# A two-layer graph network on one Trainium2 core: the load ring's 1 MB chunks moved as two transfers of 512 KB, each with its own semaphore

## The chip, the cores and the metric

The kernel runs on one core of a Trainium2 chip. The metric is the device time of one execution in microseconds (us); of several runs the median is given. Inside a core, TensorE (PE) multiplies, VectorE (DVE) and ScalarE (ACT) work on elements, GpSimd (POOL) and SyncE (SP) issue transfers here, and 16 DMA engines move data between HBM and the on-chip memory of 128 partitions.

## The reference

x is 8192 x 128, adj is a dense 8192 x 8192 matrix, all float32. Two residual graph layers are computed, and both need all of adj:

```python
# layer 0
adj_hat = adj + eye
d = 1.0 / sqrt(sum(adj_hat, axis=1))
h = relu((adj_hat * d[:, None] * d[None, :]) @ (x @ W0) + b)
x = layernorm(x + h)
# layer 1
s = x @ W1
o = relu(s + adj @ s + x @ Wself)
o = o - mean(o, axis=0)
o = o / sqrt(mean(sum(o * o, axis=1) + 1e-6))
out = layernorm(x + o)
```

Layer 0 needs the row sums of adj (for d) before it can scale the rows that it multiplies, and layer 1 needs layer 0's result.

## The kernel before

adj is cut into 8 x 8 blocks of 1024 x 1024, and each block into Q = 4 chunks of 1 MB: 128 partitions by 2048 floats, 8 KB per partition. A chunk has JB = 2 slices of 1024 columns (BLK). The host lays adj out twice, transposed within the blocks (`adjT`, for the products) and plain (`adjN`, for row sums), each chunk contiguous.

There are three kinds of chunks in one list, `chunks`, whose order every engine follows:

- "keep": a diagonal block's chunk, loaded into the tile `kept` (the memory of `o1`, so the profile calls it o). It is summed by column by VectorE (L680, L684) and later multiplied from there. It has its own semaphore per q.
- "sum": a chunk of `adjN` whose row sums are taken, by ScalarE (`sum_rows`, L497, in place with an accumulator, one instruction per slice) if `chunk.act`, else by VectorE (L670, one reduction of the whole chunk).
- "mul": a chunk of `adjT` that is multiplied. Float32 is split in two: for each slice ScalarE writes hi (L491), VectorE lo = raw - hi (L664), and TensorE runs hi and lo against the stationary halves rhi and rlo (L959, L961, L965: six matmuls of 128x512 for one layer, twelve for two), and in phase 1 four more per slice that sum columns (L941). rhi (L485) and rlo (L662) are made once per chunk. There are DEEP = 4 hi and lo tiles; ScalarE may write the hi of slice n when slice n - 4 is multiplied (semaphore slice_multiplied).

**Stages.** Stage 0 loads row block 0: 4 kept chunks and 28 sum chunks. Stage k (1 to 7) multiplies the kept chunks and column k - 1 for the rows from k on, each product chunk beside one sum chunk or kept chunk of row k, for as long as there are some, and ends with a tail of 8 product chunks (TAIL), in which the degrees of row block k are found (close_sums, L975; turn_degree, L985, which writes pA; first_product, L995). That is phase 1, up to about 780 us. Phase 2 runs blocks for both layers from one load, phase 3 (from about 1400 us) the rest of layer 1. Then the last normalisations follow.

**The ring.** Sum chunks, and product chunks that aren't kept, go through ring buffers of 1 MB: four of their own (raw0 to raw3) and, while nothing else needs that memory, s34 and s56 (in s1) and z23, z45, z67 (in zr); the profile calls these s and zr. Nine serve in stage 0 and the first stages, fewer later, four in phase 2, seven in phase 3. A planner gives each ring chunk the buffer that was freed first, `chunk.load` (how many loads that buffer has had) and `chunk.after`, the semaphore and count that say that the former chunk in the buffer is used up: ("split", n) when VectorE has made lo of n slices, ("act", n) or ("dve", n) when n sum chunks are done. SP (L419, L426) issues all adj transfers in the list's order, and waits for `after` before each. A consumer waits for `landed(chunk)`. All of SP's transfers go on DMA queue q1. GpSimd loads blocks of x transposed (512 KB, 4 KB per partition) into s1 once per stage, on queue q0.

Of the 532 adj transfers on q1, 32 are of kept chunks and 500 go through the ring.

Of the kernel before, what the change touches and what calls it, by code (L numbers as in the profile page):

```python
# [49 lines left out]
def graph_kernel(nc, x, xT, adjT, adjN, W0, b_rows, W1, Wself, out):  # L50
# [10 lines left out]
    BLK = 1024  # L61
    NB = N // BLK
    assert NB == 8
    Q = 4
    JB = 2
# [95 lines left out]
    for chunk in chunks:  # L161
        if chunk.kind == "mul":
            chunk.base = slices
            slices += JB
            chunk.stats = tuple(range(stats, stats + len(chunk.layers)))
            stats += len(chunk.layers)
            chunk.freed = ("split", slices)
            visits[chunk.visit].end = slices
        elif chunk.kind == "sum" and chunk.act:
            act_sums += 1  # L170
            chunk.freed = ("act", act_sums)
        elif chunk.kind == "sum":
            dve_sums += 1
            chunk.freed = ("dve", dve_sums)

# [6 lines left out]
    for chunk in chunks:  # L184
        if chunk.kind == "keep" or chunk.cached:
            continue
        phase = visits[chunk.visit].phase if chunk.kind == "mul" else 1
        if phase == 3 and not late:
            late = True
            free_buffers.extend((b, ("split", chunk.base)) for b in LATE)  # L190
        while phase < 3 and free_buffers[0][0] in BORROWED and (
                phase == 2 or chunk.stage > BORROWED[free_buffers[0][0]]):
            free_buffers.popleft()
        chunk.buf, chunk.after = free_buffers.popleft()
        loads[chunk.buf] += 1
        chunk.load = loads[chunk.buf]
        free_buffers.append((chunk.buf, chunk.freed))
        if phase == 1:
            phase1_last[chunk.buf] = chunk.freed
# [2 lines left out]
        for s in chunk.stats:  # L202
            stat_end[s] = chunk.base + JB
    kept_end = {(c.row, c.q): c.base + JB for c in chunks if c.cached}
    act_sums_of = [sum(1 for c in chunks if c.kind == "sum" and c.act and c.stage <= k) for k in range(NB)]


    free = {0: None, 1: None}
# [63 lines left out]
    with ctx:  # L272
# [58 lines left out]
        pD = pb("pD")  # L331
        sums = [pC, pD]

        loaded = {b: sem(f"loaded_{b}") for b in raw}
        kept_in = [sem(f"kept_in{q}") for q in range(Q)]
        consts_in = sem("consts_in")
        ident_zero = sem("ident_zero")
# [61 lines left out]
        def groups(ap):  # L399
            return ap.rearrange("p (g f) -> p g f", f=P)  # L400

        def landed(chunk):

            if chunk.kind == "keep" or chunk.cached:
                return kept_in[chunk.q], 16 * (chunk.row + 1)
            return loaded[chunk.buf], 16 * chunk.load

        def slice_of(chunk, j):
            if chunk.kind == "keep" or chunk.cached:
# [3 lines left out]
        @block.sync  # L413
        def _(sp):
            for chunk in chunks:
                if chunk.kind == "keep":
                    if chunk.row > 0:
                        sp.wait_ge(slice_split, kept_end[chunk.row - 1, chunk.q])
                    sp.dma_start(kept[:, chunk.q * TILE:(chunk.q + 1) * TILE],  # L419
                                 adjT[chunk.row, chunk.col, chunk.q]).then_inc(kept_in[chunk.q], 16)  # L420
                elif chunk.buf:
                    if chunk.after:
                        by, count = chunk.after
                        sp.wait_ge(raw_free[by], count)
                    src = adjN if chunk.kind == "sum" else adjT
                    sp.dma_start(raw[chunk.buf], src[chunk.row, chunk.col, chunk.q]).then_inc(loaded[chunk.buf], 16)  # L426

        @block.gpsimd
        def _(pool):
            pool.dma_start(w0[:, :], W0).then_inc(consts_in, 16)  # L430
            pool.dma_start(w1[:, :], W1).then_inc(consts_in, 16)
            pool.dma_start(t1[:, 0:P], Wself).then_inc(consts_in, 16)
            pool.dma_start(rows[:, :], b_rows).then_inc(consts_in, 16)
            pool.dma_start(xT_blk, xT[:, 0:BLK]).then_inc(xT_in, 16)
            pool.memset(ident[:, :], 0.0).then_inc(ident_zero, 1)
            pool.wait_ge(ident_zero, 1)
            pool.affine_select(out=ident[:, :], in_=ident[:, :], compare_op=ALU.not_equal, fill=1.0,
                               base=0, pattern=[[-1, P]], channel_multiplier=1).then_inc(ident_ready, 1)
            for k in range(1, NB):
                pool.wait_ge(y_done, k * H)  # L440
                pool.dma_start(xT_blk, xT[:, k * BLK:(k + 1) * BLK]).then_inc(xT_in, 16)
            pool.wait_ge(y_done, NB * H)
            pool.wait_ge(sums_closed, NB)
            for b in ("s34", "s56"):
                by, count = phase1_last[b]
                pool.wait_ge(raw_free[by], count)
            for k in FINAL_ROWS:
                pool.dma_start(groups(s1[:, k * BLK:(k + 1) * BLK]),
                               x[k * BLK:(k + 1) * BLK, :].rearrange("(g p) f -> p g f", p=P)).then_inc(x_in[k], 16)

            def store(k):
                pool.dma_start(out[k * BLK:(k + 1) * BLK, :].rearrange("(g p) f -> p g f", p=P),
                               groups(zr[:, k * BLK:(k + 1) * BLK])).then_inc(out_done, 16)

            def store_act(k):
                pool.wait_ge(act_normed, k + 1)
                store(k)

            def store_dve(i):
                pool.wait_ge(dve_normed, i + 1)  # L460
                store(i + NACT)

            for k in range(NACT - 1):
                store_act(k)
            for i in range(NB - NACT - 1):
                store_dve(i)
            store_act(NACT - 1)
            store_dve(NB - NACT - 1)
            pool.wait_ge(out_done, 16 * NB)

        @block.scalar
        def _(act):
            S = nc.scalar

            def split_hi(chunk):
                for l, s in zip(chunk.layers, chunk.stats):
                    src = (zr, s1)[l]
                    if l == L0:
                        act.wait_ge(z_ready, chunk.col + 1)
                    else:  # L480
                        act.wait_ge(s1_ready, ORDER[chunk.col] * H + chunk.q // 2 + 1)
                    if s >= DEEP:
                        act.wait_ge(slice_multiplied, stat_end[s - DEEP])
                    at = chunk.col * BLK + chunk.q * JB * P
                    S.activation(rhi[s % DEEP][:, :], src[:, at:at + JB * P], ACT.Copy)  # L485
                act.wait_ge(*landed(chunk))
                for j in range(JB):
                    n = chunk.base + j
                    if n >= DEEP:
                        act.wait_ge(slice_multiplied, n - DEEP + 1)  # L490
                    S.activation(hi[n % DEEP][:, :], slice_of(chunk, j), ACT.Copy).then_inc(hi_ready, 1)  # L491

            def sum_rows(chunk):
                act.wait_ge(*landed(chunk))
                for j in range(JB):
                    g = chunk.col * BG + chunk.q * JB + j
                    ins = S.activation(slice_of(chunk, j), slice_of(chunk, j), ACT.Copy,  # L497
                                       accum_out=rsum[chunk.row % 2][:, g:g + 1])
                ins.then_inc(act_summed, 1)

            def read_sums(k):
                act.wait_ge(sums_closed, k + 1)
# [132 lines left out]
        def _(dve):  # L635
# [29 lines left out]
                                 hi[n % DEEP][:, :].bitcast(f32)).then_inc(slice_split, 1)  # L665

            def sum_rows(chunk):
                dve.wait_ge(*landed(chunk))
                g = chunk.col * BG + chunk.q * JB
                V.tensor_reduce(rsum[chunk.row % 2][:, g:g + JB],  # L670
                                raw[chunk.buf].rearrange("p (g j) -> p g j", g=JB),
                                AX.X, ALU.add).then_inc(dve_summed, 1)

            def sum_kept(chunk):
                k, q = chunk.row, chunk.q
                dve.wait_ge(*landed(chunk))
                if q == 0:
                    if k > 0:
                        dve.wait_ge(sums_closed, k)
                    V.tensor_add(colsum, slice_of(chunk, 0), slice_of(chunk, 1)).then_inc(col_step, 1)  # L680
                    return
                for j in range(JB):
                    dve.wait_ge(col_step, k * (JB * Q - 1) + q * JB + j - 1)
                    V.tensor_add(colsum, colsum, slice_of(chunk, j)).then_inc(col_step, 1)  # L684
# [20 lines left out]
            def make_z(k):  # L705
# [2 lines left out]
                dk = d[:, k * BG:(k + 1) * BG]  # L708
                for b, rows in (("z23", (2, 3)), ("z45", (4, 5)), ("z67", (6, 7))):
                    if k in rows:  # L710
                        by, count = phase1_last[b]
                        dve.wait_ge(raw_free[by], count)
                step(V.reciprocal(dk, sq[:, :]))
                newton(step, dk, deg[:, :], nw[:, :])
# [386 lines left out]
```

## Time and profile before

| | us |
|---|---|
| median of 3 runs | 1932.26 |
| lowest, highest | 1929.6, 1933.44 |
| the profiled execution | 1931.12 |
| its span in the trace | 1929.3 |
| TensorE busy in it | 1742.8 (90%) |
| VectorE busy | 1522.3 (79%) |
| ScalarE busy | 1283.0 (66%) |
| adj moved on q1 | 557.88 MB in 76608 packets |

The profile is one execution on the core. Times in it are microseconds from the span's start. An engine's idle time is put down to the instruction or the landing that ended it ("<-"). The mean DMA rate is 297 GB/s, but it is spread unevenly: the page's 40 slices show 420 GB/s in most of the first eight and 131 to 200 in the middle. A timeline merges instructions that follow one another without idle time ("x2"). A packet is one piece of a transfer; a transfer over 128 partitions has 128 data packets and 16 that signal its end, one for each DMA engine, so 144.

### The profile page before, as it was taken

The numbers are of one execution on the slowest core, as the hardware profiler recorded it, in microseconds if no ns is written. First come the engines' busy times: TensorE is split into PE (matmuls) and PEld (weight loads), VectorE is DVE, ScalarE is ACT, GpSimd is POOL, SyncE is SP. The second block draws the span as 40 slices with busy tenths as digits, with TensorE's granted clock in tenths as the row PEclk, the third lists the DMA queues.
The fourth block names the chain that finished last, engine by engine and source line by source line (L and its number), as shares of the span: only waits on it lengthen the run. The fifth ranks groups of instructions, "written<-read, shape, count | busy, mean of one in ns | idle before, by whom it ended". The sixth has DMA issues, their size and how long they took to land.

```text
span 1929.3 us, 21167 instructions
## 1 busy us (share of the span) xinstructions
PE 1742.8 (90%) x7682; PEld 1411.9 (73%) x7682; DVE 1522.3 (79%) x2139; ACT 1283.0 (66%) x1885; POOL 21.5 (1%) x34
## 2 busy tenths in 40 slices
PE   1089999999999999888999999999989999999983
PEld 0068778878787877766778788788868778888872
DVE  4488688697878789975777575575589999999986
ACT  3577787677866656644554554454468888888875
POOL 0000000000000000100000000000000000000001
PEclk7589999999999999998999999999999999999995
DMA  9999999989899577743444545545579999999953
GB/s 399 421 422 421 421 370 421 401 358 389 335 373 370 198 293 320 258 175 131 173 160 168 197 159 193 194 173 189 190 292 395 354 369 381 375 376 391 375 193 87
DMA packets 80296, 572.07 MB, mean 297 GB/s; under 512 B 8960, under 2 KB 8960, under 8 KB 12096
## 3 DMA queue, kind: packets, MB, share of 16 engines
q1 hardware_dynamic: 76608, 557.88, 73.2%
q0 software_dynamic: 3584, 12.85, 2.1%
q8 instruction: 60, 0.98, 0.2%
q14 instruction: 44, 0.36, 0.0%
HBM read 566.49 MB, written 4.19 MB: 296 GB/s over the span
## 4 chain that ended last, share of the span: by engine, by line
PE 72%; DVE 15%; DMA 6%; ACT 4%; issue 2%; SPq 0%; POOL 0%; ACTq 0%
PE acc L959 20%; PE acc L961 20%; PE acc L965 20%; DVE lo L664 8%; PE pC L941 4%; DMA s<-in_adjN 4%; PE pD L941 4%; ACT hi L491 1%; DVE rlo L662 1%; DMA raw<-in_adjT 1%; DMA zr<-in_adjN 1%; DVE s L670 1%; DVE s L684 1%; PE pC L1021 1%; PE pD L1022 1%
## 5 line engine op out<-in xcount | busy, mean ns | idle before, releaser
L959 PE MATMUL acc<-hi,rhi 128*128 128x512 f32 x2048 | 823.6, 402 | 61.9 <-DVE lo L664 42.5
L961 PE MATMUL acc<-lo,rhi 128*128 128x512 f32 x2048 | 804.4, 393 | 0.0
L491 ACT ACTIVATE hi<-raw 128x1024 fp32r<-128x1024 f32 x530 | 547.3, 1055 | 143.8 <-PE pD L941 79.9
L965 PE MATMUL acc<-hi,rlo 128*128 128x512 f32 x2048 | 636.5, 392 | 0.0
L664 DVE TENSOR_TENSOR lo<-raw,hi 128x1024 fp32r<-128x1024 f32 x530 | 625.3, 1218 | 12.0 <-ACT hi L491 12.0
L959 PEld LDWEIGHTS acc<-hi,rhi 128*128 128x128 f32 x2048 | 388.2, 190 | 171.0 <-DVE lo L664 68.0
L961 PEld LDWEIGHTS acc<-lo,rhi 128*128 128x128 f32 x2048 | 388.3, 190 | 82.9 <-issue 5.0
L965 PEld LDWEIGHTS acc<-hi,rlo 128*128 128x128 f32 x2048 | 387.7, 189 | 83.0
L662 DVE TENSOR_TENSOR rlo<-zr,rhi 128x256 fp32r<-128x256 f32 x256 | 107.9, 422 | 264.5 <-ACT hi L491 264.0
L485 ACT ACTIVATE rhi<-zr 128x256 fp32r<-128x256 f32 x256 | 104.3, 407 | 197.2 <-PE acc L965 196.4
L491 ACT ACTIVATE hi<-zr 128x1024 fp32r<-128x1024 f32 x184 | 193.8, 1060 | 43.4 <-PE pD L941 22.4
L664 DVE TENSOR_TENSOR lo<-zr,hi 128x1024 fp32r<-128x1024 f32 x184 | 216.7, 1217 | 2.1 <-ACT hi L491 2.1
L662 DVE TENSOR_TENSOR rlo<-s,rhi 128x256 fp32r<-128x256 f32 x256 | 107.3, 419 | 6.4 <-ACT hi L491 4.7
L485 ACT ACTIVATE rhi<-s 128x256 fp32r<-128x256 f32 x256 | 102.7, 401 | 2.8 <-PE acc L965 2.8
L497 ACT ACTIVATE raw<-raw 128x1024 f32<-128x1024 f32 x70 | 73.0, 1045 | 30.9 <-DMA raw<-in_adjN 30.9
L491 ACT ACTIVATE hi<-s 128x1024 fp32r<-128x1024 f32 x62 | 65.3, 1059 | 38.1 <-PE pD L941 36.6
L941 PE MATMUL pC<-hi,pick 128*128 128x512 f32 x224 | 88.6, 395 | 0.0
L941 PE MATMUL pD<-hi,pick 128*128 128x512 f32 x224 | 88.2, 394 | 0.0
L941 PE MATMUL pC<-lo,pick 128*128 128x512 f32 x224 | 88.0, 393 | 0.0
L941 PE MATMUL pD<-lo,pick 128*128 128x512 f32 x224 | 87.9, 392 | 0.0
L664 DVE TENSOR_TENSOR lo<-s,hi 128x1024 fp32r<-128x1024 f32 x62 | 73.8, 1218 | 6.8 <-ACT hi L491 6.8
L491 ACT ACTIVATE hi<-o 128x1024 fp32r<-128x1024 f32 x64 | 66.2, 1053 | 16.6 <-PE pD L941 12.6
(136 smaller groups left out, 1096.4 us busy)
## 6 DMA issues: line engine op xcount, KB each, us to landing
raw<-in_adjT SPq DMA_DIRECT2D x265, 1024.0 KB, 5.0
zr<-in_adjT SPq DMA_DIRECT2D x92, 1024.0 KB, 6.0
raw<-in_adjN SPq DMA_DIRECT2D x53, 1024.0 KB, 16.4
o<-in_adjT SPq DMA_DIRECT2D x32, 1024.0 KB, 11.0
s<-in_adjT SPq DMA_DIRECT2D x31, 1024.0 KB, 12.6
zr<-in_adjN SPq DMA_DIRECT2D x30, 1024.0 KB, 19.3
s<-in_adjN SPq DMA_DIRECT2D x29, 1024.0 KB, 18.5
s<-in_xT POOLq DMA_DIRECT2D x8, 512.0 KB, 7.7
```

The lines of the kernel that those rows point to most:

```text
L485: S.activation(rhi[s % DEEP][:, :], src[:, at:at + JB * P], ACT.Copy)
L491: S.activation(hi[n % DEEP][:, :], slice_of(chunk, j), ACT.Copy).then_inc(hi_ready, 1)
L497: ins = S.activation(slice_of(chunk, j), slice_of(chunk, j), ACT.Copy, accum_out=rsum[chunk.row % 2][:, g:g + 1])
L662: V.tensor_sub(rlo[s % DEEP][:, :], (zr, s1)[l][:, at:at + JB * P], rhi[s % DEEP][:, :].bitcast(f32))
L664: V.tensor_sub(lo[n % DEEP][:, :], slice_of(chunk, j), hi[n % DEEP][:, :].bitcast(f32)).then_inc(slice_split, 1)
L670: V.tensor_reduce(rsum[chunk.row % 2][:, g:g + JB], raw[chunk.buf].rearrange("p (g j) -> p g j", g=JB), AX.X, ALU.add).then_inc(dve_summed, 1)
L684: V.tensor_add(colsum, colsum, slice_of(chunk, j)).then_inc(col_step, 1)
L941: last = T.matmul(sums[h][:, :], to, mov[n % DEEP][:, h * HALF:(h + 1) * HALF], start=False, stop=False, skip_group_check=True)
L959: T.matmul(banks[h][:, :], a, hi[n % DEEP][:, part], start=(opens and j == 0), stop=False, skip_group_check=True)
L961: T.matmul(banks[h][:, :], a, lo[n % DEEP][:, part], start=False, stop=False, skip_group_check=True)
L965: last = T.matmul(banks[h][:, :], b, hi[n % DEEP][:, part], start=False, stop=end, skip_group_check=True)
L1021: T.matmul(pC[:, j * P:j * P + P], t2[:, j * P:j * P + P], w1[:, :], start=True, stop=True)
```

## The change

Each ring chunk is now moved by two transfers of 128x1024 floats, 512 KB, 4 KB per partition, one for each slice. Each half of each buffer has a semaphore of its own (`loaded[buf, j]`). `chunk.after` and `chunk.freed` become one entry per slice: SP waits for the slice that stood in that half before it issues the half. For product chunks the first half is freed when VectorE has made lo of its first slice. ScalarE's sums signal after each slice, so counts of act_summed double. VectorE's reduction still takes the whole chunk: it waits for both halves, and frees both at its end. ScalarE waits for a half in front of each slice, where it waited once per chunk. Kept chunks, their semaphores, and the order of `chunks` are as before.

```diff
-            chunk.freed = ("split", slices)
+            chunk.freed = tuple(("split", chunk.base + j + 1) for j in range(JB))
...
-            act_sums += 1
-            chunk.freed = ("act", act_sums)
+            act_sums += JB
+            chunk.freed = tuple(("act", act_sums - JB + j + 1) for j in range(JB))
...
-            chunk.freed = ("dve", dve_sums)
+            chunk.freed = (("dve", dve_sums),) * JB
...
-        loaded = {b: sem(f"loaded_{b}") for b in raw}
+        loaded = {(b, j): sem(f"loaded_{b}_{j}") for b in raw for j in range(JB)}
...
-                    if chunk.after:
-                        by, count = chunk.after
-                        sp.wait_ge(raw_free[by], count)
                     src = adjN if chunk.kind == "sum" else adjT
-                    sp.dma_start(raw[chunk.buf], src[chunk.row, chunk.col, chunk.q]).then_inc(loaded[chunk.buf], 16)
+                    for j in range(JB):
+                        if chunk.after:
+                            by, count = chunk.after[j]
+                            sp.wait_ge(raw_free[by], count)
+                        part = slice(j * BLK, (j + 1) * BLK)
+                        sp.dma_start(raw[chunk.buf][:, part],
+                                     src[chunk.row, chunk.col, chunk.q][:, part]).then_inc(loaded[chunk.buf, j], 16)
...
-                act.wait_ge(*landed(chunk))
                 for j in range(JB):
+                    act.wait_ge(*landed(chunk, j))
                     n = chunk.base + j
...
             def sum_rows(chunk):
-                act.wait_ge(*landed(chunk))
                 for j in range(JB):
+                    act.wait_ge(*landed(chunk, j))
...
-                ins.then_inc(act_summed, 1)
+                    ins.then_inc(act_summed, 1)
...
             def sum_rows(chunk):
-                dve.wait_ge(*landed(chunk))
+                for j in range(JB):
+                    dve.wait_ge(*landed(chunk, j))
```

SP's queue in stage 1, where products (in_adjT) and sums (in_adjN) alternate; s1 and zr are the borrowed buffers. Before:

```order
L426 DMA raw0<-in_adjT 128x2048 [waits slice_split]
L426 DMA raw1<-in_adjN 128x2048 [waits slice_split]
L426 DMA raw2<-in_adjT 128x2048 [waits slice_split]
L426 DMA raw3<-in_adjN 128x2048 [waits slice_split]
L426 DMA s1<-in_adjT 128x2048 [waits act_summed]
```

and in the changed kernel:

```order
L428 DMA raw0<-in_adjT 128x1024 [waits slice_split] x2
L428 DMA raw1<-in_adjN 128x1024 [waits slice_split] x2
L428 DMA raw2<-in_adjT 128x1024 [waits slice_split] x2
L428 DMA raw3<-in_adjN 128x1024 [waits slice_split] x2
L428 DMA s1<-in_adjT 128x1024 [waits act_summed] x2
```

The order is the same; each row has become two transfers of half the width, each behind a wait of its own.

ScalarE in stage 1, a product chunk, a sum chunk and the next product chunk. Before:

```order
L485 ACTIVATE rhi0<-zr 128x256 [waits slice_multiplied,z_ready]
L491 ACTIVATE hi0<-raw0 128x1024 [waits slice_multiplied,loaded_raw0]
L491 ACTIVATE hi1<-raw0 128x1024 [waits slice_multiplied]
L497 ACTIVATE raw1,s1<-raw1 128x1024 [waits loaded_raw1]
L497 ACTIVATE raw1,s1<-raw1 128x1024
L485 ACTIVATE rhi1<-zr 128x256 [waits slice_multiplied,z_ready]
L491 ACTIVATE hi2<-raw2 128x1024 [waits slice_multiplied,loaded_raw2]
```

and in the changed kernel:

```order
L488 ACTIVATE rhi0<-zr 128x256 [waits slice_multiplied,z_ready]
L494 ACTIVATE hi0<-raw0 128x1024 [waits slice_multiplied,loaded_raw0_0]
L494 ACTIVATE hi1<-raw0 128x1024 [waits slice_multiplied,loaded_raw0_1]
L500 ACTIVATE raw1,s1<-raw1 128x1024 [waits loaded_raw1_0]
L500 ACTIVATE raw1,s1<-raw1 128x1024 [waits loaded_raw1_1]
L488 ACTIVATE rhi1<-zr 128x256 [waits slice_multiplied,z_ready]
L494 ACTIVATE hi2<-raw2 128x1024 [waits slice_multiplied,loaded_raw2_0]
```

No instruction moves; each second slice has a wait on its own half.

## Rows read from the trace of the kernel before

**Rows 1.** Busy time by stretch; the columns are in the first line.

```profile
core 0: us, PE busy (x) PEld busy (x) DVE busy (x) ACT busy (x) POOL busy (x), PEclk, DMA share, GB/s
...
144.70:193.00 48.30, 48.17 (x211) 39.10 (x210) 38.94 (x41) 37.22 (x56) 0.00 (x0) 1.00 1.01 420
...
241.00:289.00 48.00, 44.36 (x192) 35.56 (x191) 40.87 (x48) 38.85 (x60) 0.53 (x1) 1.00 0.90 369
...
1000.00:1350.00 350.00, 345.59 (x1560) 283.72 (x1559) 222.22 (x381) 175.33 (x289) 0.00 (x0) 1.00 0.49 180
...
1400.00:1830.00 430.00, 417.37 (x1818) 338.92 (x1817) 421.64 (x520) 369.87 (x475) 0.00 (x0) 0.99 0.94 367
```

**Rows 2.** ScalarE in order of time: start, us, what, idle before and its end.

```profile
169.57 2.01 ACT L491 ACTIVATE hi<-raw 128x1024 fp32r<-128x1024 f32 x2 [2.65 <-DMA raw<-in_adjT]
...
209.31 2.01 ACT L491 ACTIVATE hi<-raw 128x1024 fp32r<-128x1024 f32 x2 [2.66 <-DMA raw<-in_adjT]
...
211.80 2.01 ACT L491 ACTIVATE hi<-raw 128x1024 fp32r<-128x1024 f32 x2 [0.17 <-DMA raw<-in_adjT]
```

**Rows 3.** The chain that ended last, 190 to 211 us: start, us, what.

```profile
190.46 18.83 DMA raw<-in_adjT
209.31 1.07 ACT hi L491
210.41 0.42 DVE rlo L662
210.83 1.15 DVE lo L664
```

**Rows 4.** DMA queues, 94 to 102, then 50 to 100 us: packets, MB, share.

```profile
q1 hardware_dynamic: 391, 2.83, 85.1%
q0 software_dynamic: 144, 0.52, 16.4%
...
q1 hardware_dynamic: 2815, 20.55, 98.8%
q0 software_dynamic: 144, 0.52, 2.6%
```

**Rows 5.** DMA queue and issues of kept chunks, 0 to 209.3 us.

```profile
q1 hardware_dynamic: 11760, 85.71, 98.7%
...
o<-in_adjT SPq DMA_DIRECT2D x8, 1024.0 KB, 14.9
```

**Rows 6.** Lone transfers: 645 to 665, 718 to 730, 260 to 268 us.

```profile
q1 hardware_dynamic: 432, 3.15, 42.9%
...
q0 software_dynamic: 144, 0.52, 14.7%
...
s<-in_adjT SPq DMA_DIRECT2D x1, 1024.0 KB, 4.8
```

**Rows 7.** SP's issues in order of time: start, us, what, count.

```profile
6.09 7.01 SPq L426 DMA_DIRECT2D zr<-in_adjN  x3
...
203.19 0.33 SPq L426 DMA_DIRECT2D s<-in_adjN  x1
```

**Rows 8.** The DMA queue from 268 to 336.5 us, and ScalarE at its end.

```profile
q1 hardware_dynamic: 3853, 28.16, 99.4%
...
336.46 1.06 ACT L491 ACTIVATE hi<-raw 128x1024 fp32r<-128x1024 f32 x1 [1.50 <-DMA raw<-in_adjT]
```

**Rows 9.** The DMA queue, 1500 to 1800 us, and TensorE at 1600 us.

```profile
q1 hardware_dynamic: 15286, 111.34, 94.9%
...
1599.87 0.39 PE L959 MATMUL acc<-hi,rhi 128*128 128x512 f32 x1
...
1601.23 0.39 PE L959 MATMUL acc<-hi,rhi 128*128 128x512 f32 x1
```

**Rows 10.** Who waited for whom, 640 to 780 us: total, times, longest.

```profile
ACT hi L491 <- DMA raw<-in_adjT: 7.3, 4, 2.4
...
PE acc L959 <- DVE lo L664: 1.2, 4, 0.5
```

More of the change, by code:

```diff
@@ L189, in graph_kernel @@
             late = True
-            free_buffers.extend((b, ("split", chunk.base)) for b in LATE)
+            free_buffers.extend((b, (("split", chunk.base),) * JB) for b in LATE)
         while phase < 3 and free_buffers[0][0] in BORROWED and (
@@ L204, in graph_kernel @@
     kept_end = {(c.row, c.q): c.base + JB for c in chunks if c.cached}
-    act_sums_of = [sum(1 for c in chunks if c.kind == "sum" and c.act and c.stage <= k) for k in range(NB)]
+    act_sums_of = [sum(JB for c in chunks if c.kind == "sum" and c.act and c.stage <= k) for k in range(NB)]
     free = {0: None, 1: None}
@@ L400, in groups, with landed @@
             return ap.rearrange("p (g f) -> p g f", f=P)
-        def landed(chunk):
+        def landed(chunk, j):
             if chunk.kind == "keep" or chunk.cached:
                 return kept_in[chunk.q], 16 * (chunk.row + 1)
-            return loaded[chunk.buf], 16 * chunk.load
+            return loaded[chunk.buf, j], 16 * chunk.load
         def slice_of(chunk, j):
@@ L444, in _ @@
             for b in ("s34", "s56"):
-                by, count = phase1_last[b]
+                by, count = phase1_last[b][-1]
                 pool.wait_ge(raw_free[by], count)
@@ L675, in sum_kept @@
                 k, q = chunk.row, chunk.q
-                dve.wait_ge(*landed(chunk))
+                dve.wait_ge(*landed(chunk, 0))
                 if q == 0:
@@ L710, in make_z @@
                     if k in rows:
-                        by, count = phase1_last[b]
+                        by, count = phase1_last[b][-1]
                         dve.wait_ge(raw_free[by], count)
```

## The prediction

> **What bounds the kernel now.** I read the table by stretches first [rows 1]. From 145 to 193 us, as in every stretch up to 241 us, the DMA engines are full: a share of 1.01 at 420 GB/s, which is 1.0486 MB every 2.49 us. From 241 to 289 us the share is 0.90 [rows 1], and from there on the DMA engines are full only for a while in each stage. From 1000 to 1350 us the DMA share is 0.49 and TensorE is busy for 345.59 of 350 us; from 1400 to 1830 us TensorE (417 of 430 us) and VectorE (422) are full, and DMA has 0.94 [rows 1].
>
> A full DMA does not yet mean that the end waits for it, so I read next what ScalarE, the first consumer of most chunks, waits for. From 150 to 209 us it stands at a product chunk once in 19.9 us for 2.65 us, and it is always the landing that ends the wait [rows 2]; 169.57 to 209.31 us is 39.74 us for 16 chunks, 2.48 us each, the pace of the DMA. The chain of waits agrees: a landing issued at 190.46 us is followed by hi, rlo and lo of that slice, and so by TensorE [rows 3]. The wait at 211.80 us is 0.17 us [rows 2] and is the last one of stage 1. So the time up to 209.3 us is the DMA's, and later TensorE's and VectorE's chains carry it. What the change does to the time is read from these first 209 us.
>
> **The price of a smaller transfer.** Every ring transfer had 8 KB per partition; now two have 4 KB each, in 128 pieces plus 16 completions each (144 packets in both cases). The kernel already has transfers of exactly the new shape: x^T, 512 KB in rows of 4 KB, which lands among ring transfers. From 94 to 102 us, q0's 144 packets took 16.4% of 16 x 8 us, 20.99 engine-us; over 16 engines 1.312 us, 2.624 us for a pair. q1's 391 packets took 85.1%, 108.9 engine-us, so 144 of them took 2.507 us per engine [rows 4]. The difference is +0.117 us per chunk. From 50 to 100 us the same working gives 2.60 against 2.527 us, +0.073 us, and the rounding of the 2.6% makes that +0.02 to +0.125 [rows 4]. I take +0.09 us per chunk, between the two, and keep 0.02 and 0.125 as ends. Below nothing the price can't be, since the same bytes go in more packets. The far end is a lone transfer: from 718 to 730 us q0's 144 packets took 14.7% of 192 us, 3.53 us for a pair, where three lone 8 KB transfers took 2.86 us each [rows 6]; a lone transfer's first pieces take long, and that goes away in a stream, as 2.86 against 2.507 shows, so I give this end no weight in the sum.
>
> The Trainium skill (DMA: Bandwidth & Descriptors, section "Why small descriptors are slow") has about 3 cycles of overhead per packet, at the 850 MHz that the page states. Eight more data packets per engine would then be 28 ns per chunk by this estimate, near the lower end of the rows, and the delay below would be 2.1 us instead of 6.7.
>
> **How many chunks pay.** By 209.3 us q1 had moved 85.71 MB, 81.7 transfers of 1.0486 MB, and 8 of them are kept chunks, which are not split [rows 5]: 73.7 ring chunks. 73.7 x 0.09 = 6.6 us later landing of the chunk on which TensorE hangs at 209.3 us.
>
> **What half a chunk earlier gives back.** The chunk's first half now lands one half, 2.58/2 = 1.29 us, ahead of its second. ScalarE makes hi of the first slice at once, and TensorE at 212 us hangs on just that slice [rows 3]. The second slice is in time: it comes 1.29 us behind, while the first takes TensorE 2.3 us (ten matmuls at about 0.23 us, by the pace of [rows 9]). So 1.3 us comes back, once, since the waits before it are one and the same bound. Net: 6.6 - 1.3 = +5.3 us.
>
> **Buffers freed by the slice** (SP waits for half a buffer). As long as the DMA queue never runs empty, an earlier issue lands nothing earlier: 0 until 209 us. Behind that, what SP waits for is a slot, and consumers wait for landings almost nowhere, so it is 0 there too; it is what could cover part of the next point.
>
> **The second full stretch.** From 268 to 336.5 us the DMA is at 99.4% again and moved 28.16 MB, 26.9 chunks, 4 of them kept [rows 8]. At 336.46 us ScalarE waits 1.50 us for a landing [rows 8]. 22.9 x 0.09 = 2.1 us later, less 1.3 us for the half: 0.8 us more wait. TensorE doesn't see it: ScalarE may start hi when the slice four back is multiplied, which leaves three slices of 2.3 us, 6.9 us, for a chain of hi, rlo and lo of 1.07 + 0.42 + 1.15 us [rows 3]; that is a cover of 4.2 us, of which 1.50 is used. 0 us.
>
> **The last phase.** TensorE's slices start 1.36 us apart (1599.87 and 1601.23 us), 2.72 us per chunk [rows 9]; the DMA would need 2.58. From 1500 to 1800 us it moved 111.34 MB [rows 9], 106 chunks in 300 us, one in 2.83 us on the mean. The cover is 0.14 us per chunk within a run of slices, which the chunks in store bridge, and 0.25 us on the mean, gone only at a price of 0.34 us. 0 us.
>
> **Issues and waits.** SP issues 500 transfers more. An issue takes 0.33 us in the steady part [rows 7], two in 2.58 us. The eleventh to thirteenth of the first issues take 7.01 us together without a wait on a semaphore [rows 7]: SP is held when some ten transfers are outstanding. Twice the transfers for the same bytes reach that at half the bytes, about 5 MB, which is still 13 us of work for the DMA; what is held behind it on SP (kept chunks too) could not land earlier anyway. 0 us. ScalarE gets one wait more per chunk, on a landing that in TensorE's part is long past: its two hi of a chunk already have a passed wait between them, and none of their starts pays for it. The sums of ScalarE signal per slice instead of per chunk, as hi does already. VectorE's sums wait for both halves, and free nothing earlier. 0 us for each.
>
> **Sum.** The profiled execution took 1931.12 us (span 1929.3); +5.3 gives 1936.4. It lies 1.1 us under the median of 1932.26, so the forecast on the median is 1937.6 us, +0.27%.
>
> **Rivals.**
> A, not slower: the price of a packet in a full stream is at the low end, 0.02 to 0.065 us per chunk. 1.5 to 4.8 us less 1.3: +0.2 to +3.5, 1932.5 to 1935.8 us, 1934 in the middle. For it: the rounding of the 2.6% row [rows 4]. Against it: the narrower window, 0.117. It decides at (3.9 + 1.3)/73.7 = 0.07 us.
> B, faster: the low price, and the half landing pays where the ring is short. From 640 to 780 us ScalarE waits for landings four times, 7.3 us in all [rows 10]; if each were on the path, 4 x 1.3 = 5.2 us come back, 1927 to 1931 us. Against it: TensorE waits for VectorE's lo there for 1.2 us in all [rows 10], so little can be had.
> C, slower by more: the full stretches of stages 2 to 4 start with less data in store, and each adds its own 2.1 us: +2 to +6 on top, 1940 to 1944 us. It decides when the cover of 2.7 us at 336 us is gone. Against it: stage 2's extra wait is worked out at 0.8 us.
> D: the price is over 0.34 us and the last phase runs at the DMA's pace; at 0.45 the first 209 us cost 73.7 x 0.45 - 1.3 = 32 us, and the 164 chunks of the last phase 0.11 each, 18 more: about 1982 us. Against it: both windows of [rows 4].
> E: what a transfer costs beyond its bytes is not hidden. A lone 1 MB lands 4.8 us after its issue [rows 6] and takes 2.49 in the stream; if each of the 74 added transfers cost the 2.3 us between them, 170 us: 2100 us. The Trainium skill (DMA: Bandwidth & Descriptors, "Rules for kernel authors") says the like: at least 1 MiB per DMA for full bandwidth. Against it: nine transfers are outstanding in the stretch that matters, and the 512 KB transfers in [rows 4] show no such gap.
>
> **How the numbers follow.** Forecast 0.55, A 0.25, C 0.11, B 0.05, D 0.03, E 0.01. The range takes in A and the forecast's upper end (0.125 x 73.7 - 1.3 = +7.9, 1940.2) and C: 1932 to 1944 us. A measurement of this kernel tells about 0.2%, 3.9 us, from no change. Above 1936.1 us lie C, D, E and most of the forecast (0.50): 0.65. Within are A and the rest: 0.30. Faster 0.05.
>
> **What would show it.** In the changed kernel's profile: 421 GB/s of the first 240 us down to about 406; the landing that frees TensorE at the end of stage 1 at 214 to 216 us instead of 209.3; the step to pA (the degree turned) of stage 1 some 5 us later, and the same 5 us at each later stage, neither growing nor shrinking; issues of SP of 1.3 us each in the first 200 us. A bandwidth that stays at 421 GB/s would make me wrong towards A; a shift that grows from stage to stage, towards C; waits of ScalarE for landings behind 1400 us, towards D.

## The result, and the profile after

| | before | changed |
|---|---|---|
| median, us (8 runs each) | 1931.74 | 1936.61 |
| lowest to highest | 1929.6 to 1937.13 | 1935.84 to 1938.64 |
| span of the profiled execution | 1929.3 | 1934.9 |

The ratio is 1.0024, with a 95% interval of 1.0013 to 1.0035: 4.9 us slower, where +5.3 was forecast. The profiled spans differ by 5.6 us.

The same stretches of the changed kernel, with the columns of [rows 1]:

```profile
144.70:193.00 48.30, 46.69 (x196) 35.94 (x196) 36.94 (x41) 35.85 (x53) 0.00 (x0) 1.00 1.03 409
...
241.00:289.00 48.00, 44.29 (x201) 35.82 (x200) 39.87 (x48) 40.87 (x65) 0.53 (x1) 1.00 0.94 372
...
1000.00:1350.00 350.00, 345.59 (x1562) 283.68 (x1561) 222.55 (x382) 177.11 (x293) 0.00 (x0) 1.00 0.55 180
...
1400.00:1830.00 430.00, 415.95 (x1817) 337.70 (x1816) 419.35 (x517) 366.91 (x473) 0.00 (x0) 1.00 0.97 364
```

Up to 241 us the DMA engines are as full as before, with a share of 1.03, but move 409 GB/s instead of 420. TensorE is busy 46.69 of the 48.3 us from 144.7 us on, where it was 48.17 [rows 1]. In the last phase the DMA share rises from 0.94 to 0.97 at nearly the same rate; TensorE's busy time in that window differs by 1.4 us, with all its work shifted by some 5 us.

ScalarE in stage 1 of the changed kernel, answering to [rows 2] (start, us, what, idle before and what ended it):

```profile
173.43 1.06 ACT L494 ACTIVATE hi<-raw 128x1024 fp32r<-128x1024 f32 x1 [2.48 <-DMA raw<-in_adjT]
...
214.37 1.06 ACT L494 ACTIVATE hi<-raw 128x1024 fp32r<-128x1024 f32 x1 [2.47 <-DMA raw<-in_adjT]
215.65 1.06 ACT L494 ACTIVATE hi<-raw 128x1024 fp32r<-128x1024 f32 x1 [0.22 <-DMA raw<-in_adjT]
...
218.19 1.06 ACT L494 ACTIVATE hi<-raw 128x1024 fp32r<-128x1024 f32 x1 [0.19 <-DMA raw<-in_adjT]
```

and the chain that ended last there (start, us, what), answering to [rows 3]:

```profile
198.37 15.97 DMA raw<-in_adjT
...
214.37 1.07 ACT hi L494
...
215.46 0.43 DVE rlo L665
215.89 1.15 DVE lo L667
```

The landing that frees TensorE at the end of stage 1 has moved from 209.31 to 214.37 us, +5.06. The second half is waited for at 215.65 us, 1.28 us behind the first. The chain behind the first half is the one of [rows 3], with the same durations.

How the 5 us go on is read from the step that writes pA (the degree turned) near the end of a stage. Stages 1, 2, 3 and 7, before, in order of time (start, us, what):

```profile
227.79 1.84 PE L985 MATMUL pA<-ident,t 128*128 128x1 f32 x16
...
358.21 1.84 PE L985 MATMUL pA<-ident,t 128*128 128x1 f32 x16
...
470.33 1.84 PE L985 MATMUL pA<-ident,t 128*128 128x1 f32 x16
...
774.77 1.84 PE L985 MATMUL pA<-ident,t 128*128 128x1 f32 x16
```

and in the changed kernel:

```profile
232.84 1.84 PE L989 MATMUL pA<-ident,t 128*128 128x1 f32 x16
...
363.33 1.84 PE L989 MATMUL pA<-ident,t 128*128 128x1 f32 x16
...
477.09 1.84 PE L989 MATMUL pA<-ident,t 128*128 128x1 f32 x16
...
781.75 1.84 PE L989 MATMUL pA<-ident,t 128*128 128x1 f32 x16
```

The shifts are 5.05, 5.12, 6.76 and 6.98 us; at the end of the span it is 5.6. So nearly all is there by the end of stage 1. The 1.6 us that come in stage 3 and go again behind 780 us are of the clock; they have a part of their own below.

The price of the pieces: queue q1 and the 512 KB transfer on q0 from 94 to 102 us, then q1 in the full stretch from 20 to 95 us, changed, and last the same stretch before (packets, MB, share):

```profile
q1 hardware_dynamic: 756, 2.74, 85.7%
q0 software_dynamic: 144, 0.52, 16.6%
...
q1 hardware_dynamic: 8430, 30.72, 102.6%
...
q1 hardware_dynamic: 4343, 31.65, 101.4%
```

A transfer of 144 packets on q1 takes 0.857 x 128 / 756 x 144 / 16 = 1.306 us per engine, 2.61 us for a pair; the estimate from x^T's rows had been 2.60 to 2.62 [rows 4]. But the bytes came down by less than the packets' times: 30.72 against 31.65 MB in 75 us is a chunk in 2.56 instead of 2.485 us, +0.075 us, while the sum of packet times over the engines rose from 101.4% to 102.6% of the stretch. A sum over 100% means that packets of one engine overlap, and the shorter ones overlap a little more.

SP's issues in stage 0 of the changed kernel (start, us, what, count):

```profile
24.09 10.20 SPq L428 DMA_DIRECT2D raw<-in_adjN  x8
...
46.82 10.20 SPq L428 DMA_DIRECT2D raw<-in_adjN  x8
```

Eight issues take 10.20 us, 1.28 each, one landing: SP is held at its queue, as [rows 7] had shown for the first issues. The landings come in an unbroken stream all the same.

### The profile page after: what moved, and what is told of

Read it like the earlier page. It is cut to its first block, busy times and chain, and to the rows that moved or that the text cites. A ratio compares the mean times of both kernels' runs of the same rounds, so it can differ in the third digit from the quotient of the medians.

```text
span 1934.9 us, 22120 instructions
## 1 busy us (share of the span) xinstructions
PE 1739.9 (90%) x7682; PEld 1406.6 (73%) x7682; DVE 1523.0 (79%) x2139; ACT 1285.8 (66%) x1885; POOL 21.5 (1%) x34
## 4 chain that ended last, share of the span: by engine, by line
PE 68%; DVE 18%; DMA 8%; ACT 3%; issue 2%; SPq 1%; POOL 0%; ACTq 0%; DVEq 0%
PE acc L963 19%; PE acc L969 19%; PE acc L965 19%; DVE lo L667 9%; PE pC L945 4%; PE pD L945 4%; DMA raw<-in_adjT 3%; DMA raw<-in_adjN 3%; DVE rlo L665 1%; DVE s L688 1%; ACT hi L494 1%; DMA s<-in_adjN 1%; DMA zr<-in_adjN 1%; DVE s L674 1%; DVE ux L731 1%
## 5 line engine op out<-in xcount | busy, mean ns | idle before, releaser
L494 ACT ACTIVATE hi<-o 128x1024 fp32r<-128x1024 f32 x64 | 66.1, 1053 | 16.7 <-PE pD L945 12.6
## 6 DMA issues: line engine op xcount, KB each, us to landing
raw<-in_adjN SPq DMA_DIRECT2D x106, 512.0 KB, 15.2
zr<-in_adjN SPq DMA_DIRECT2D x60, 512.0 KB, 15.2
s<-in_adjN SPq DMA_DIRECT2D x58, 512.0 KB, 15.2
```

## Experiments

Two theories stood against each other. **P**: pieces of 4 KB land more slowly than pieces of 8 KB, the DMA's stream up to 215 us carries that to the end, and the half that is used early gives about a microsecond back. **N**: the number of transfers, with their end signals, issues and waits, is the price. Beside them, **L**: part of the price is paid in later stages. All ratios are against the kernel before, run on the same chip beside it; its medians there were 1932.5 us (runs 1 to 3), 1930.8 us (runs 4 and 8) and 1930.1 us (the rest). Beside the times stand places in one trace of each run. How far such a place scatters by itself can be read from runs 5 and 6, which repeat the first two stages of the changed kernel and of the kernel before: pA of stage 1 differs by 0.27 and 0.16 us from theirs.

**1. The change's transfers, consumed in whole chunks.** ScalarE waits for both halves, and both are freed at the chunk's end:

```diff
-            chunk.freed = tuple(("split", chunk.base + j + 1) for j in range(JB))
+            chunk.freed = (("split", slices),) * JB
...
                 for j in range(JB):
                     act.wait_ge(*landed(chunk, j))
+                for j in range(JB):
                     n = chunk.base + j
```

> The changed kernel's transfers (two of 512 KB for a ring chunk), but consumed as before: ScalarE waits for both halves before its first slice, and both halves are freed together at the chunk's end. Theory P (smaller pieces land more slowly, and half a chunk's earlier start gives 1.28 us back): nothing of the delay is given back, so +6.3 us on the kernel before, about 1938, with TensorE's gating hi of stage 1 at 215.6 us instead of 214.4. Rival G (slice-wise waits and frees are worth nothing, the +5 is all the transfers' price): same as the changed kernel, 1936.6. Rival W (the extra waits and signals cost the time, not the transfers): near the kernel before, under 1934.

Measured: 1.0022 (1.0014 to 1.0031), 1937.1 us. Its chain at the end of stage 1 (start, us, what):

```profile
197.94 15.93 DMA raw<-in_adjT
213.86 1.35 issue
215.22 1.07 ACT hi L495
...
216.31 0.43 DVE rlo L667
216.74 1.15 DVE lo L669
```

The first half has landed at 213.86 us, and hi starts 1.35 us later, at 215.22 us, when the second half is there. TensorE's slice follows at 217.93 us, against 217.08 in the changed kernel and 212.02 before [rows 3]. So the transfers alone cost 5.9 us at this place, and using the half early gave 0.85 us back. Run 5, whose first two stages are the changed kernel's, gives a second reading of that:

```profile
214.08 1.06 ACT L508 ACTIVATE hi<-raw 128x1024 fp32r<-128x1024 f32 x1 [2.47 <-DMA raw<-in_adjT]
215.36 1.06 ACT L508 ACTIVATE hi<-raw 128x1024 fp32r<-128x1024 f32 x1 [0.22 <-DMA raw<-in_adjT]
...
216.79 0.50 PE L977 MATMUL acc<-hi,rhi 128*128 128x512 f32 x1 [0.16 <-DVE lo L681]
```

Its TensorE starts this slice at 216.79 us, 1.14 us before run 1. So the half is worth 0.85 to 1.14 us, more than the scatter. The time is 4.2 us over the kernel before (2.7 to 6.0), less than the 6.3 expected; it can't tell 1.0022 from the change's 1.0024, so rival G falls by the traces alone. Rival W, under 1934 us, falls here by the time, and again in run 2, which has neither the waits nor the signals.

**2. One transfer of 1 MB per chunk, but in pieces of 4 KB.** The host lays adj out slice by slice, and the transfer picks both slices:

```diff
-                    sp.dma_start(raw[chunk.buf], src[chunk.row, chunk.col, chunk.q]).then_inc(loaded[chunk.buf], 16)
+                    sp.dma_start(raw[chunk.buf].rearrange("p (j c) -> p j c", j=JB),
+                                 src[chunk.row, chunk.col, chunk.q].rearrange("j p c -> p j c")).then_inc(loaded[chunk.buf], 16)
```

> The kernel before with one transfer of 1 MB and one wait per ring chunk, but with adj laid out in HBM slice by slice, so that each piece is 4 KB as in the change (kept chunks as before). Theory P: the size of the pieces is the price: full stretches at about 410 GB/s instead of 421, 73.7 chunks at +0.07 us, nothing given back: +5 to +6 us, 1937 to 1938. Rival N (the number of transfers, their end signals and SP's held issues are the price): 421 GB/s as before and +0, 1931.7.

Measured: 1.0022 (1.0013 to 1.0031), 1937.1 us. Its queue q1 from 20 to 95 us, and two landings that ScalarE waits for, sixteen chunks apart:

```profile
q1 hardware_dynamic: 7963, 30.71, 102.6%
...
173.94 2.01 ACT L492 ACTIVATE hi<-raw 128x1024 fp32r<-128x1024 f32 x2 [2.81 <-DMA raw<-in_adjT]
...
214.86 2.01 ACT L492 ACTIVATE hi<-raw 128x1024 fp32r<-128x1024 f32 x2 [2.82 <-DMA raw<-in_adjT]
```

30.71 MB in 75 us, as in the changed kernel, with half as many transfers and end signals (7963 packets instead of 8430). 40.92 us for 16 chunks is 2.558 us each, where [rows 2] give 39.74 us, 2.484 each: +0.074 us. The landing that gates TensorE is at 214.86 us, 5.55 us late; 73.7 chunks x 0.074 is 5.45. So the price comes without a second transfer: P stands, N falls. With two transfers the chunk is there at 215.22 (run 1), 215.36 (run 5) and 215.65 us (the changed kernel), 0.36 to 0.8 us later than here, although q1 has moved 83.33 to 83.39 MB by 209.3 us in all four. Up to 0.3 us of that is scatter. Whether the rest is a small price of the second transfer, no run with pieces of 4 KB settles; run 4, with pieces of 8 KB, has none. This trace also has the shift without the clock's part: its pA comes 5.53, 5.53, 5.49 and 5.49 us late in stages 1, 2, 3 and 7.

**3. Two transfers with pieces of 8 KB, lower and upper 64 partitions.**

```diff
-                    sp.dma_start(raw[chunk.buf], src[chunk.row, chunk.col, chunk.q]).then_inc(loaded[chunk.buf], 16)
+                    for j in range(JB):
+                        part = slice(j * (P // JB), (j + 1) * (P // JB))
+                        sp.dma_start(raw[chunk.buf][part, :],
+                                     src[chunk.row, chunk.col, chunk.q][part, :]).then_inc(loaded[chunk.buf, j], 16)
```

> The kernel before with each ring chunk in two transfers of 64 partitions, pieces of 8 KB as before, both waited for before the chunk is used, freed as a whole. Theory P: only the second set of 16 end signals is added; 420 to 421 GB/s in the full stretches, within 1 us of the kernel before. Rival N (the number of transfers): +5 to +6 us, about 410 GB/s.

Measured: six runs from 2444 to 2555 us, median 2487.5; the ratio of the three shortest is 1.275 (1.269 to 1.281), and the profiled one took 2542.8 us. Neither theory had that. From 20 to 95 us:

```profile
DMA packets 2529, 16.62 MB, mean 222 GB/s; under 512 B 501, under 2 KB 501, under 8 KB 501
...
q1 hardware_dynamic: 2529, 16.62, 101.7%
```

222 GB/s, with the engines as full as ever: 1.017 x 1200 us over 2028 pieces (2529 packets less 501 end signals) is 0.60 us a piece of 8 KB. The Trainium skill (SBUF — State Buffer, section "Door 1: The DMA port swizzle") says that the rate of a transfer depends on how many of the 16 ways into the memory its partitions reach, and by its table the lower 64 reach eight, with about 218 GB/s as their limit; the trace agrees within 2%, with 222. This run can't judge N; run 4 answers both questions.

**4. The same with even and odd partitions.**

```diff
-                        part = slice(j * (P // JB), (j + 1) * (P // JB))
+                        part = slice(j, P, JB)
```

> As the run with two transfers of 64 partitions each, but one takes the even and the other the odd partitions, instead of the lower and the upper half; pieces of 8 KB, both waited for. It answers what that run could not, whether a second transfer costs anything by itself. Theory U (there the pieces took twice as long because a transfer to one half of the partitions reaches half of the ways into the memory): here a piece takes 314 ns again, 420 GB/s, and the time is within 1.5 us of the kernel before (1930 to 1933). Rival M (two transfers of 64 partitions are slow as such, by how they are dealt to the 16 engines): about 2490 again. If the pieces are fine and it still comes out 5 us slower, the number of transfers has a price of its own.

Measured: 1.0001 (0.9991 to 1.0011), 1930.6 us. From 20 to 95 us:

```profile
DMA packets 4819, 31.62 MB, mean 422 GB/s; under 512 B 960, under 2 KB 960, under 8 KB 960
...
q1 hardware_dynamic: 4817, 31.60, 101.3%
```

422 GB/s, 0.315 us a piece of 8 KB (1215.6 us over 3857 pieces), with 960 end signals in place of 480. So two transfers of the same bytes cost nothing if their pieces stay at 8 KB, which speaks against N a second time, and rival M falls: what was wrong with the halves by partition was which partitions they were, not that there were two. By the table of the Trainium skill (SBUF — State Buffer, section "Door 1: The DMA port swizzle") each of these transfers reaches all sixteen ways. The rows read from HBM change together with the partitions, and no run parts the two.

**5. The change in stages 0 and 1 alone; 6. from stage 2 on alone.** A flag `chunk.cut` (its negation in run 6) chooses per chunk between the two halves and one whole transfer that is waited for and freed as before:

```diff
+        chunk.cut = chunk.kind != "mul" and chunk.stage <= 1 or chunk.kind == "mul" and 0 < chunk.stage <= 1
...
+                    if not chunk.cut:
+                        if chunk.after:
+                            by, count = chunk.after[-1]
+                            sp.wait_ge(raw_free[by], count)
+                        sp.dma_start(raw[chunk.buf],
+                                     src[chunk.row, chunk.col, chunk.q]).then_inc(loaded[chunk.buf, 0], 16)
+                        continue
```

> The change for the ring chunks of stages 0 and 1 alone; from stage 2 on, ring chunks move as one transfer of 1 MB, waited for and freed whole. Theory P: the whole price lies in the first 215 us: +5 us, 1936.6, with every later stage shifted by the same 5. Rival L (part of the price lies in the later full stretches of stages 2 to 4 or in the last phase): +2 to +4.

> The change for the ring chunks from stage 2 on alone. Theory P: no difference from the kernel before, within 1 us (1931 to 1932.5), since no landing gates TensorE behind 215 us: the waits of ScalarE that are left (2.5 us at 343 us in the changed kernel) are covered. Rival L: +1 to +3 us.

Measured: early alone 1.0029 (1.0017 to 1.0040), 1936.3 us; late alone 1.0004 (0.9995 to 1.0013), 1932.0 us. In the trace of the first the writes of pA are at 232.57, 363.05 and 476.80 us, +4.8, +4.8 and +6.5; the second has 227.95, 360.05, 472.29, that is +0.2, +1.8 and +2.0. Of the +6.5, and of the +1.8 and +2.0, 1.6 us are again the clock's (below). Run 6 has them in stage 2, where its granted clock is 0.94 and that of the kernel before 1.00 (columns of [rows 1]):

```profile
265.00:292.00 27.00, 25.22 (x102) 20.23 (x103) 23.33 (x24) 19.76 (x30) 0.00 (x0) 0.94 0.88 341
```

80 chunks are cut in run 5 and the other 420 in run 6. The pieces of the 420 cost the DMA engines time too, from 1000 to 1350 us 55.6% of it, where it was 48.8%, for the same 62.9 MB; no landing of theirs carries it to the end. So L falls by the traces: of the 2.2 us at pA of stage 7, 0.6 are left without the clock's part. The time alone would not exclude 1 to 2 us of it: run 6's interval reaches from -1.0 to +2.5 us.

**7. Four transfers of 256 KB per chunk**, pieces of 2 KB, two transfers to a half's semaphore:

```diff
+                        for h in range(H):
+                            part = slice(j * BLK + h * HALF, j * BLK + (h + 1) * HALF)
+                            sp.dma_start(raw[chunk.buf][:, part],
+                                         src[chunk.row, chunk.col, chunk.q][:, part]).then_inc(loaded[chunk.buf, j], 16)
```

> The change carried on: four transfers of 256 KB per ring chunk, 2 KB per partition, one semaphore per half. Theory P with a fixed price per piece: from 8 to 16 pieces per engine and chunk cost 0.075 us, so 32 pieces cost 0.22 in all: 74 x 0.22 = 16.5 us, less 1.3: +15 us, 1947, with 395 to 398 GB/s in the full stretches; the last phase needs 2.83 us per chunk and gets 2.71, so nothing is added there. Rival S (SP's issues, 0.33 us each and held when about ten transfers are outstanding, become the limit): over +25 us, and gaps in the full stretches. Rival H (the price is one of the second transfer, not of the pieces): +5 to +8.

Measured: 1.0097 (1.0083 to 1.0111), 1949.8 us: 18.7 us slower, where 15 were expected. q1 from 20 to 95 us, and a piece of the chain in stage 2:

```profile
q1 hardware_dynamic: 15907, 28.98, 105.3%
...
350.00 9.85 DMA raw<-in_adjT
359.87 1.07 ACT hi L495
```

28.98 MB in 75 us is 386 GB/s, 2.71 us a chunk: +0.23 us over the kernel before, as expected from a fixed price per piece (0.075 for 8 pieces more per engine and chunk, 0.225 for 24). The 395 to 398 GB/s of the expectation don't follow from its own price, which gives 388. Rivals S and H fall, the time lying between them and the stretch having no gap. pA is written at 244.50 us in stage 1, 16.7 us late; expected was 15.2. What had been left out is the second line of the chain: in stage 2 a landing gates TensorE again, at 359.87 us. That is rival C of the prediction, at three times the change's price. At 378.34 us stage 2 is 20.1 us late, 1.6 of the 3.4 between them being the clock's (below).

**8. Quarters in stages 0 and 1 alone.** The edit of 7 under the flag of 5.

> Four transfers of 256 KB per ring chunk in stages 0 and 1 alone, whole chunks from stage 2 on. With quarters everywhere the degree turned was 16.7 us late at the end of stage 1 and 20.1 at the end of stage 2. Theory C2 (the second full stretch came to gate TensorE there, by its own price of 0.2 us per chunk): the 3.4 us between the two are gone, except where a stretch at half clock falls in between (1.5 us); stage 1 at 244.5 us, stage 2 at 374.9 to 376.5, in all 1946.5. Rival (the loss behind stage 1 is of the clock or of the shifted meeting of the engines alone): stage 2 at 378 again, 1949.5.

Measured: 1.0099 (1.0084 to 1.0114), 1949.9 us; that total, 3.4 us over the expected one, can't be told from that of run 7. In the trace pA is written at 243.96 us in stage 1 and at 376.00 in stage 2, as expected, and no landing is waited for in between. Stage 2 takes 132.04 us here and 133.84 with quarters throughout, both with one stretch at half clock in them: the gating landing of stage 2 costs 1.8 us. The spans, 1947.2 against 1948.8 us, say the same; the timed runs are too few to.

**9. Only six chunks in halves**, the last two product chunks before the column sums close in stages 1 to 3 (the flag of 5 with another condition).

> The kernel before, with the change for six chunks alone: the last two product chunks before the column sums close in stages 1, 2 and 3, among them the one whose landing gates TensorE at 209.3 us. Theory P: the gating slice starts 1.24 us earlier and almost nothing is paid: -1.2 us, 1930.5. That is less than a measurement of the time can tell; the trace shows it: the hi at 209.31 us at 208.1, and the degree turned (writing pA) at 226.7 instead of 227.95. Rival G (the half is worth nothing): both as before.

Measured: 1.0003 (0.9994 to 1.0012). hi of the gating chunk and TensorE's first matmul on it (start, us, what):

```profile
208.29 1.06 ACT L508 ACTIVATE hi<-raw 128x1024 fp32r<-128x1024 f32 x1 [1.64 <-DMA raw<-in_adjT]
...
211.84 0.50 PE L977 MATMUL acc<-hi,rhi 128*128 128x512 f32 x1
```

hi starts 1.0 us earlier than at 209.31 [rows 2], but TensorE only 0.2 us earlier than at 212.02: pA is written at 227.60 instead of 227.79 us. TensorE was still at the slices before. Before this landing it had waited only for the 0.2 us between their end at 211.8 and 212.02, since its pace of 4.6 us for a product chunk is close to the DMA's 4.97 us for a product and a sum chunk. The expected 1.2 us were wrong; a lone half is worth what TensorE waits at that landing, not what the half lands ahead. With 0.16 us of scatter in pA, the 0.2 us gained can't be told from rival G.

No version beats the kernel before.

## Why the prediction was right, point by point

**What bounds the first 209 us.** Right: a slower stream came out as a later end, by 5.05 us at pA of stage 1, and the change in stages 0 and 1 alone makes the whole loss (run 5).

**The price of a piece.** The packets' own times were right (2.61 us a pair, 2.60 to 2.62 forecast), the price was a bit too high: 0.09 forecast, 0.070 by the rates of 409.5 and 421 GB/s, 0.074 by the landings of run 2. The step that was off is the division by 16 engines as if packets stood in line: they overlap, by 1.4% before and 2.6% after. The 3 cycles per packet of the Trainium skill (DMA: Bandwidth & Descriptors, section "Why small descriptors are slow"), 28 ns per chunk by the estimate in the prediction, would have given 0.8 us in all; 70 to 75 ns were measured, so here the measurement decides against it.

**The chunks that pay.** 73.7 fits: times 0.074 it is 5.45 us, and run 2 has 5.55, run 1 5.91 at the same place. Forecast were 6.6.

**What the half gives back.** Forecast 1.3 us, measured 0.85 (run 1 against the change) to 1.14 (run 1 against run 5). The first half does land 1.28 us ahead of the second. But the second half of the changed kernel lands at 215.65 us, that of run 5 at 215.36 and that of run 1 at 215.22, with the same 83.33 MB moved by 209.3 us in each. So the stream isn't slower: the 0.4 us are mostly the scatter of single landings, 0.29 us between the first two, which share this part of the program. Run 9 corrects the reason that the prediction gave, that TensorE hangs on the one slice at 212 us: it had waited 0.2 us for it, and the last halves alone gave no more. That the gain comes about because all product chunks are early, so that TensorE has no backlog of its own, fits runs 1 and 9 but wasn't tried by itself.

The forecast's +5.3 against 5.05 there is closer than its terms. Against run 1 the price is 0.7 us too high (6.6 for 5.91) and the half 0.45 too high (1.3 for 0.85), and the two errors partly cancel; that much of the closeness is luck. The median came out 1.0 us under the 1937.6 forecast, half of it because the kernel before has a median of 1931.74 over eight runs, where the forecast started from 1932.26.

**The second full stretch.** The wait was to grow from 1.50 us by 0.8; it is 2.46 us:

```profile
342.99 1.06 ACT L494 ACTIVATE hi<-raw 128x1024 fp32r<-128x1024 f32 x1 [2.46 <-DMA raw<-in_adjT]
```

and stage 2's shift is 5.12 us against stage 1's 5.05, so it stayed covered. Run 7 shows the cover's end: at a price of 0.23 us per chunk it is gone, and costs 1.8 us. By the prediction's own terms, 2.7 us of cover plus the 1.3 of the half over 22.9 chunks, it is gone at 0.17 us.

**The last phase.** ScalarE waits for no landing from 780 to 1830 us, as before. q1 moved 111.58 MB from 1500 to 1800 us against 111.34 [rows 9]:

```profile
q1 hardware_dynamic: 30647, 111.58, 98.7%
```

Its share rose from 94.9% to 98.7%, and no landing was waited for. With quarters (run 7) it is 103.8% there, and ScalarE waits for a landing twice from 780 to 1830 us, 2.8 us in all.

**Issues and waits.** The held issues were seen as foretold and cost nothing; run 4 has the issues doubled at no loss.

**Rivals.** A needed a price under 0.07 us, which it nearly has. The time says slower (4.9 us, interval 2.5 to 6.8), but the interval reaches into A's +0.2 to +3.5; what excludes A is the 5.05 us in the trace. B to E didn't come. One sign that the prediction named was misleading: "a shift that grows from stage to stage" was to point to C, and the shift did grow, by 1.6 us in stage 3, for another reason.

## What the runs showed that was not expected

**TensorE's clock adds or takes 1.6 us by stage.** From 401 to 411 us of the changed kernel, just behind the short stalls in which each stage begins, the granted clock is 0.83 on the mean; then 1.00. Busy times by stretch, with the columns of [rows 1]:

```profile
401.00:411.00 10.00, 8.22 (x30) 6.29 (x29) 9.70 (x12) 8.52 (x14) 0.00 (x0) 0.83 0.60 209
411.00:417.00 6.00, 6.00 (x28) 4.99 (x27) 3.00 (x4) 5.23 (x8) 0.00 (x0) 1.00 1.03 429
```

and the matmuls in it, four in order of time:

```profile
407.17 0.63 PE L945 MATMUL pC<-hi,pick 128*128 128x512 f32 x1
407.59 0.63 PE L945 MATMUL pC<-lo,pick 128*128 128x512 f32 x1
...
410.47 0.39 PE L945 MATMUL pC<-hi,pick 128*128 128x512 f32 x1
410.69 0.39 PE L945 MATMUL pC<-lo,pick 128*128 128x512 f32 x1
```

Two successive starts are 0.42 us apart at 407 us (the level of 1.2 GHz) and 0.22 to 0.23 us at 410 us (2.4 GHz). The kernel before has no such stretch there, but has one behind 836 us, where the changed kernel has none. Before, then changed:

```profile
836.00:846.00 10.00, 7.37 (x30) 5.49 (x28) 5.79 (x8) 5.70 (x10) 0.00 (x0) 0.88 0.55 210
```

```profile
843.00:852.00 9.00, 5.79 (x28) 4.26 (x26) 6.39 (x9) 5.97 (x10) 0.00 (x0) 1.00 0.68 237
```

TensorE is 5.18 us behind the kernel before at 405.08 us, ahead of the slow matmuls, and 6.75 us behind at 411.37. That is why the shift goes from 5.12 to 6.76 us in stage 3, and from 6.98 us at 805 us to 5.40 at 846 (the two additions into t, at 805.32 and 845.88 us before, 812.30 and 851.28 changed). Runs 6 to 9 have a clock under 1 between 269 and 290 us instead, and a shift of 1.6 us there. In the traces before and after, TensorE had stood idle just ahead of this place in a stage three times for VectorE's lo, 0.6 to 1.8 us each, whether the clock then fell or not. What decides whether the clock falls at such a place wasn't tried, nor whether the change has a part in it: the changed kernel and runs 1 and 5 have it in stage 3, run 2 doesn't, with one trace each. A difference of 1.6 us that appears at one place of a trace is not to be read as an effect of a change until the granted clock there has been looked at; here it was a third of the effect.

**Transfers to the lower and upper 64 partitions in turn run at half the rate**, 222 GB/s against 422 with every second partition (runs 3 and 4), though sixteen engines are busy in both.

## What to carry to other kernels

In a stretch in which the DMA engines are full, count pieces, not transfers: here a piece cost some 9 ns beyond its bytes (0.075 us for 8 more per engine and chunk), so halving a row of 8 KB cost 3% of the rate, and 32 pieces in place of 8 cost 8 to 9%. A second transfer that kept the pieces whole cost nothing when it took every second partition (run 4), and a piece took twice the time when the two took the lower and the upper half (run 3). Using data by the half pays only where a consumer waits for landings with nothing of its own queued; behind a full stream it gave back about 1 us once, less than half a chunk, while the price was paid by every chunk up to the last landing that gates.
